# Fourier stage of a two-layer decoder kernel: VectorE reads a group's queries two units into the group, PE turns and projects the next group one unit sooner

## Chip, cores and metric

The kernel runs on one core of one Trainium2 chip. The metric is the device time of one execution in microseconds (us), as the median of several runs; lower is better. One further execution was taken with the hardware profiler, and all rows and views below come from that one.

## What is computed

A decoder of two layers on 64 sequences of 64 tokens of width 128. Layer 0 is self-attention, cross-attention and a mixture of experts, layer 1 is an attention with Fourier features, a latent cross-attention and a ternary feed-forward block; after each stands a layer norm over `x + branch(x)`. The change touches only the Fourier attention of layer 1, which has 16 heads of 8 numbers:

```
def _fourier_kernel(x, proj_mat):
    p = jnp.einsum('blhd,dm->blhm', x, proj_mat) / math.sqrt(D_HEAD)
    return jnp.concatenate([jnp.cos(p), jnp.sin(p)], axis=-1) / math.sqrt(D_KMAP)
q = (x @ Wq.T + bq).reshape(Bv, Lv, N_HEAD, D_HEAD)
k = (x @ Wk.T + bk).reshape(Bv, Lv, N_HEAD, D_HEAD)
v = (x @ Wv.T + bv).reshape(Bv, Lv, N_HEAD, D_HEAD)
q_prime = _fourier_kernel(q, proj_mat)
k_prime = _fourier_kernel(k, proj_mat)
kv = jnp.einsum('blhm,blhd->bhmd', k_prime, v)
out = jnp.einsum('blhm,bhmd->blhd', q_prime, kv)
out = out.reshape(Bv, Lv, D_MODEL)
return out @ Wo.T + bo
```

## The kernel before

The 4096 tokens stand in SBUF as 32 tiles of 128 tokens. The Fourier stage takes them in G = 8 groups of T = 4 tiles (512 tokens, that is 8 sequences). Each engine runs its own instruction list, written out in Python loops, and the lists meet only at semaphores; within an engine the order of the list is the order of execution.

The work of a group is cut into UPG = 16 **units** of 128 x 1024 angles: n = 0 to 7 (KEYS = 8) are the keys' features, n = 8 to 15 the queries'. All loops run over N = 16 g + n. For each unit the stations are:

- PE, `angles(N)` (L895 for keys, L897 for queries): the projection onto 128 random directions, into one of two pairs of PSUM banks. The PE loop issues it two units ahead, in iteration N - 2; it waits until VectorE has reduced unit N - 2, because that unit had the same banks.
- VectorE, `reduce_(N)`: the fractional part of the angle in turns. For ten units of a group this is `f_whole` (L1258), `f_frac` (L1266) and `f_wrap` (L1268). For the six units of `ON_SCALAR = (2, 5, 7, 10, 12, 14)` ScalarE rounds (`lift`, L1090, tile `f_lifted`), and VectorE does only `f_frac` (L1263) and `f_wrap`.
- ScalarE, `features(N)`: a sine (L1082) and a cosine (L1086). A `lift(N + 2)` stands between the two.
- PE again: `key_values` (L916) sums features times values over the keys' units, `turn_key_values` (L948) turns the sums, `outputs(g, q)` (L961) multiplies the queries' features with them, and `combine(g - 1)` (L975), in iteration n = 2 of the next group, is the output projection, which VectorE adds to the stream in `residual` (L1275) at n = 4.

Beside these, each group has to be prepared while the one before it is at work:

- `columns_of(g + 1)` on PE (L860): four transposes of the normalised tokens `f_xs` into bank 6, copied by ScalarE to `f_xT` (L1062). In both loops this stands at n = 11. After the transposes GpSimd is free to fill `f_xs` for the group after that (L1391) and to add the output bias to the stream (L1395).
- `keys_and_values(g + 1)` on PE at n = 12 (L867 and L869), read by VectorE after `reduce_` at n = 13: `keys` (`f_kT`, L1234) and `values` (`f_vS`, L1242).
- `queries(g + 1)` on PE at n = 14 (L874), behind `outputs(g, 2)`, read by VectorE after `reduce_` at n = 15 (`f_qT`, L1249). What `queries` writes is first used by PE in `angles` at n = 8 of group g + 1, which PE issues in its iteration n = 6:

```
if n == KEYS:
    pe.wait_ge(s["q_sb"], g + 1)
```

The keys' bank and the queries' bank are the same, bank 7; the next to write into it is `turn_key_values` at n = 6 of group g + 1, after that wait. SyncE has one DMA in the stage that depends on the queries: it waits until the last group's `queries` matmul has run, and then loads the first rows of the context into `f_xT`. Neither the DMA nor the matmul it waits for is touched.

In the names used below, unit (g, n) or "unit 13" is a unit of the loops above, and "reduced" means that `f_frac` of that unit is done.

Of the kernel before, what the change touches and what calls it, by code (L numbers as in the profile page):

```python
# [29 lines left out]
G = NT // T  # L30
# [679 lines left out]
def experts_and_fourier_phase(nc, ctx, c, name):  # L710
# [15 lines left out]
    KEYS = T * KU  # L726
# [42 lines left out]
    def x_bank(g):  # L769
        return XT if g == 0 else 6  # L770
# [22 lines left out]
    with nc.Block() as block:  # L793
# [8 lines left out]
        def _(pe):  # L802
# [50 lines left out]
            def columns_of(g):  # L853
                pe.wait_ge(s["staged"], g + 1)
                if g >= 1:
                    pe.wait_ge(s["kvT_sb"], 2 * g)
                else:
                    pe.wait_ge(e["xT_sb"], G)
                for t in range(T):
                    last = nc.tensor.transpose(ps[:, x_bank(g), t * P:(t + 1) * P], xs[:, t, :], ident)  # L860
                last.then_inc(s["xT_ps"], 1)
# [10 lines left out]
            def queries(g):  # L872
                pe.wait_ge(s["k_sb"], g + 1)
                nc.tensor.matmul(ps[:, k_bank(g), :], w("f_wq"), xT[:, :], start=True, stop=True).then_inc(s["q_ps"], 1)  # L874

            def angles(N):
                g, n = divmod(N, UPG)
                if n == 0:
                    pe.wait_ge(s["k_sb"], g + 1)
                if n == KEYS:  # L880
                    pe.wait_ge(s["q_sb"], g + 1)
                if N == 0:
                    pe.wait_ge(s["v_sb"], 1)
                    pe.wait_ge(s["q_sb"], 1)
                if N == 1:
                    pe.wait_ge(e["relued"], PIECES - 2)
                if N >= 2:
                    pe.wait_ge(s["reduced"], N - 1)
                for q in range(2):
                    out = ps[:, 2 * (N % 2) + q, :]  # L890
                    rows = slice(S * q, S * q + S)
                    if n < KEYS:
                        t, u = divmod(n, KU)
                        h = 8 * q + 4 * u
                        last = nc.tensor.matmul(out, kT[rows, t * P:(t + 1) * P], projX[rows, h:h + 4, :], start=True, stop=True)  # L895
                    else:
                        last = nc.tensor.matmul(out, projX[rows, n - KEYS + 8 * q, :], qT[rows, :], start=True, stop=True)  # L897
                last.then_inc(s["z_ps"], 1)

            def key_values(N):  # L900
                g, n = divmod(N, UPG)
                t, u = divmod(n, KU)
                if n == 0:
                    pe.wait_ge(s["v_sb"], g + 1)
                    if g >= 1:
                        pe.wait_ge(s["o_sb"], g * Q4 - 1)
                    else:
                        pe.wait_ge(e["relued"], PIECES)
                if n == 1 and g >= 1:
                    pe.wait_ge(s["o_sb"], g * Q4)  # L910
                if t == 2 and u == 0:
                    pe.wait_ge(s["kv_sb"], 2 * g + 1)
                pe.wait_ge(s["feats"], N + 1)
                for place in range(8 * u, 8 * u + 8):
                    q, r = divmod(place, 4)
                    last = nc.tensor.matmul(ps[32 * r:32 * r + 32, 4 + q // 2, (q % 2) * 256:(q % 2 + 1) * 256],  # L916
                                            vS[:, t % 2, t // 2, head_of(place), :],
                                            feats[:, n % RING, place % 2 * 4 + place % 8 // 2, :, :],
                                            start=(t % 2 == 0 and q % 2 == 0), stop=(t % 2 == 1 and q % 2 == 1))
                last.then_inc(s["kv_ps"], 1)  # L920
# [60 lines left out]
            for m in range(PIECES + 2):  # L981
                g, i = divmod(m, PARTS)
# [19 lines left out]
            for N in range(ALL + 5):  # L1002
                g, n = divmod(N, UPG)
                if N + 2 < ALL:
                    angles(N + 2)
                if g < G:
                    if 1 <= n <= KEYS:
                        key_values(N - 1)
                    if 3 <= N <= 6:
                        latent_products(N - 3)  # L1010
                    if n == (8 if g == 0 else 6):
                        turn_key_values(g, 0)
                    if n == 9:
                        turn_key_values(g, 1)
                    if n >= KEYS + 2 and n % 2 == 0:
                        outputs(g, n // 2 - 5)
                    if g + 1 < G:
                        if n == 11:
                            columns_of(g + 1)
                        if n == 12:  # L1020
                            keys_and_values(g + 1)
                        if n == 14:
                            queries(g + 1)
                if g >= 1:
                    if n == 0:
                        outputs(g - 1, Q4 - 1)
                    if n == 2:
                        combine(g - 1)

        @block.scalar  # L1030
        def _(act):
# [24 lines left out]
            def root(n, tiles):  # L1056
                act.wait_ge(e["variances"], n)
                nc.scalar.activation(rstd[:, tiles], rstd[:, tiles], ACT.Sqrt).then_inc(e["roots"], 1)
# [60 lines left out]
            for m in range(PIECES):  # L1119
                g, i = divmod(m, PARTS)  # L1120
# [11 lines left out]
            for N in range(ALL + 5):  # L1132
                g, n = divmod(N, UPG)
                if g < G:
                    if N == KEYS:
                        act.wait_ge(s["ab_ps"], 4)
                        act.wait_ge(e["lowered"], PIECES)
                        act.wait_ge(e["measured"], 2 * G)
                    if N == KEYS - 2:
                        root(3, LATE)  # L1140
                    features(N)
                    if 3 <= N <= 6:
                        keep_products(N - 3)
                    if n == 4:
                        keep_kv(g, 0)
                    if g == 0 and n == 8:
                        keep_turned(g, 0)
                    if n == 8:
                        keep_kv(g, 1)
                    if g >= 1 and n == 7:  # L1150
                        keep_turned(g, 0)
                    if n == 9:
                        keep_turned(g, 1)
                    if n >= KEYS + 3 and n % 2 == 1:
                        keep_o(g, (n - KEYS - 3) // 2)
                    if n == 11 and g + 1 < G:
                        columns_of(g + 1)
                if g == G and n == 0:
                    act.wait_ge(s["var"], 1)
                    nc.scalar.activation(c["rstd"][:, 0:MEASURED], c["rstd"][:, 0:MEASURED], ACT.Sqrt)  # L1160
                    nc.scalar.activation(rstdc[:, :], rstdc[:, :], ACT.Sqrt).then_inc(s["root"], 1)
                if g >= 1:
                    if n == 1:
                        keep_o(g - 1, Q4 - 1)
                if g == G and n == 2:
                    act.wait_ge(s["var2"], 1)
                    nc.scalar.activation(rstd2[:, 0:MEASURED], rstd2[:, 0:MEASURED], ACT.Sqrt).then_inc(s["root2"], 1)

        @block.vector
        def _(dve):  # L1170
# [76 lines left out]
            def queries(g):  # L1247
                dve.wait_ge(s["q_ps"], g + 1)
                nc.vector.tensor_scalar(qT[:, :], ps[:, k_bank(g), :], turn_scale, qb[:, :], ALU.mult, ALU.add).then_inc(s["q_sb"], 1)  # L1249
# [82 lines left out]
            for m in range(PIECES):  # L1332
                g, i = divmod(m, PARTS)
# [20 lines left out]
            for N in range(ALL + 6):  # L1354
                g, n = divmod(N, UPG)
                if N == 1:
                    e_residual(G - 1)
                if N == 3:
                    dve.wait_ge(e["measured"], 2 * G)
                    variance(LATE)  # L1360
                if N == KEYS:
                    inverse_of_root(3, LATE)
                if g == G and n == 0:
                    variances()
                    scales()
                    first_latents()
                if g < G:
                    reduce_(N)
                    if g + 1 < G:
                        if n == KEYS + 5:  # L1370
                            keys(g + 1)
                            values(g + 1)
                        if n == KEYS + 7:
                            queries(g + 1)
                if g >= 1 and n == 4:
                    residual(g - 1)

# [838 lines left out]
```

## Time and profile before

| | |
|---|---|
| median of 3 runs | 1605.61 us (1602.69 to 1608.95) |
| the profiled execution, its own time | 1600.41 us |
| its span, first to last instruction | 1598.6 us |
| mean granted TensorE clock | 0.969 of full speed |
| busy share of the span: PE, VectorE, ScalarE, GpSimd | 89%, 71%, 60%, 19% |
| Fourier stage | about 500 to 930 us |

The shares of the whole span mix five stages. The Fourier stage has to be read by itself: by the time from one group to the next, and by which engine waits for which inside a group. In the rows, an entry such as "[0.82 <-PE psum L867]" says that the engine sat idle for 0.82 us before this instruction until the PE instruction of line 867 released it. PE names TensorE's matmuls, PEld its weight loads, DVE is VectorE, ACT ScalarE, POOL GpSimd. In a timeline the printed durations of two neighbours overlap by some 0.1 us; the distance of two starts is the better measure. A row of busy times gives the stretch and its length, then for PE, PEld, DVE, ACT and POOL the busy microseconds with the number of instructions, then the mean granted TensorE clock, the DMA engines' busy share and GB/s.

### The profile page before, as it was taken

Reading aid. Unit: us, or ns where it says so; the run is one execution under the profiler, and the core shown is the slowest. Engines: PE = TensorE matmul, PEld = TensorE weight load, DVE = VectorE, ACT = ScalarE, POOL = GpSimd, SP = SyncE. Lnnn points to the kernel's source line nnn. Section 1 sums busy time; section 2 is a strip of 40 time slices with the busy share of each in tenths; the row PEclk is TensorE's granted clock in tenths of the full one; section 3 lists DMA queues with packets and bytes.
Section 4 is the critical chain, followed back from the end, with each engine's and each line's share of the span. In section 5 each row is a group of like instructions: output and inputs, shape, how many; then the busy total and the mean of one; then the engine's idle time right before and its main releaser. Section 6 shows DMA issues by size and latency. Waiting matters only on the chain. (4 is left out here: it accounts for less than half of the span.)

```text
span 1598.6 us, 32271 instructions
## 1 busy us (share of the span) xinstructions
PE 1420.6 (89%) x12643; PEld 867.7 (54%) x12658; DVE 1135.5 (71%) x2367; ACT 959.8 (60%) x1494; POOL 303.4 (19%) x278
## 2 busy tenths in 40 slices
PE   6999999997999788878887878999999999999962
PEld 4666666665665333334333354666666666666541
DVE  4666778886336799889988944355677767766788
ACT  2333367666555988789878954445666655565433
POOL 3434334452001100111010031111222111110101
PEclk9999999998999999999999989999999999999995
DMA  4000000001000000000000002222222222222310
GB/s 179 2 2 2 2 19 12 15 6 54 1 1 1 1 2 1 1 1 1 1 1 4 1 14 56 70 65 62 57 60 66 68 67 66 61 57 57 72 45 17
DMA packets 41013, 50.78 MB, mean 32 GB/s; under 512 B 9248, under 2 KB 23200, under 8 KB 40480
## 3 DMA queue, kind: packets, MB, share of 16 engines
q1 hardware_dynamic: 40576, 48.06, 11.7%
q8 instruction: 102, 1.67, 0.5%
q10 hardware_dynamic: 288, 0.67, 0.1%
q14 instruction: 47, 0.39, 0.1%
HBM read 13.04 MB, written 2.10 MB: 9 GB/s over the span
## 5 line engine op out<-in xcount | busy, mean ns | idle before, releaser
L1852 DVE TENSOR_TENSOR l_px<-psum,l_share 128x1024 f32<-128x1024 f32 x64 | 78.4, 1225 | 157.9 <-PE psum L1554 104.2
L1702 ACT ACTIVATE l_prob<-psum,l_bias 128x1024 f32<-128x1024 f32 x64 | 71.3, 1114 | 173.6 <-PE psum L1529 173.6
L1541 PE MATMUL psum<-l_XT,l_A 128*128 128x256 f32 x512 | 127.1, 393 | 1.0 <-ACT l_XT L1720 1.0
L1524 PE MATMUL psum<-l_th,l_XT 128*128 128x512 f32 x256 | 124.0, 607 | 1.9 <-issue 0.7
L1592 PE MATMUL psum<-l_px,l_N 128*128 128x256 f32 x512 | 124.0, 385 | 1.8 <-ACT l_r L1746 1.8
L1554 PE MATMUL psum<-l_prob,l_X 128*128 128x512 f32 x256 | 123.1, 603 | 0.0
L895 PE MATMUL psum<-f_projX,f_kT 64*128 64x512 f32 x256 | 75.2, 664 | 34.1 <-DVE f_frac L1266 18.6
L1592 PEld LDWEIGHTS psum<-l_px,l_N 128*128 128x128 f32 x512 | 93.9, 191 | 19.0 <-issue 4.7
L1833 DVE TENSOR_REDUCE l_top<-psum 128x8 bf16<-128x1024 f32 x64 | 78.1, 1221 | 36.4 <-PE psum L1609 36.4
L1541 PEld LDWEIGHTS psum<-l_XT,l_A 128*128 128x128 f32 x512 | 94.9, 195 | 12.4 <-ACT l_XT L1720 1.4
L1266 DVE TENSOR_TENSOR f_frac<-psum,f_whole 128x1024 f32<-128x1024 f32 x80 | 98.0, 1225 | 2.7
L1258 DVE TENSOR_SCALAR f_whole<-psum 128x1024 f32<-128x1024 f32 x80 | 97.4, 1217 | 1.8 <-PE psum L895 1.3
L2051 POOL TENSOR_TENSOR l_hn<-l_hh,late_weights 128x1024 f32<-128x1024 f32 x16 | 37.6, 2351 | 307.1 <-DVE l_hh L1910 307.1
L1707 ACT COPY l_th<-psum 128x1024 f32<-128x1024 f32 x64 | 64.8, 1012 | 47.7 <-PE psum L1541 47.7
L1268 DVE TENSOR_SCALAR f_wrap<-f_frac 128x1024 int32<-128x1024 int32 x128 | 89.9, 702 | 4.4
L408 ACT ACTIVATE a_probT<-psum 128x1024 f32<-128x1024 f32 x32 | 32.7, 1023 | 96.4 <-PE psum L199 96.4
L916 PE MATMUL psum<-f_feats,f_vS 128*32 128x256 f32 x1024 | 70.3, 393 | 15.1 <-ACT f_feats L1086 7.9
L961 PE MATMUL psum<-f_qf,f_kvm 128*32 128x256 f32 x1024 | 70.6, 422 | 13.3 <-ACT f_kvm L1114 6.7
L669 POOL TENSOR_TENSOR a_KX<-a_KT,const 128x1024 f32<-128x1024 f32 x32 | 60.8, 1903 | 113.6 <-ACT a_KT L375 89.5
L1082 ACT ACTIVATE f_feats<-f_frac 128x1024 f32<-128x1024 f32 x64 | 67.6, 1056 | 23.2 <-DVE f_frac L1266 23.2
L480 DVE TENSOR_TENSOR a_prob<-psum,relbias 128x1024 f32<-128x1024 f32 x32 | 39.2, 1225 | 55.6 <-PE psum L185 50.1
L399 ACT ACTIVATE c_QX<-c_QT,const 128x128 f32<-128x128 f32 x256 | 78.5, 403 | 0.0
(310 smaller groups left out, 3177.5 us busy)
## 6 DMA issues: line engine op xcount, KB each, us to landing
l_share<-l_recip SPq DMA_DIRECT2D x512, 64.0 KB, 2.0
early_weights<-in_weights SPq DMA_DIRECT2D x1, 2405.0 KB, 11.3
c_cs<-in_ctx SPq DMA_DIRECT2D x16, 128.0 KB, 2.1
f_qf<-in_l_mats SPq DMA_DIRECT2D x1, 2048.0 KB, 7.8
out<-l_normed SPq DMA_DIRECT2D x16, 128.0 KB, 2.0
l_craw<-in_ctx SPq DMA_DIRECT2D x15, 128.0 KB, 2.3
late_weights<-in_weights SPq DMA_DIRECT2D x1, 1089.0 KB, 11.2
relbias<-in_relbias ACTq DMA_DIRECT2D x1, 512.0 KB, 5.2
```

Source lines behind the costliest of these rows:

```text
L399: last = nc.scalar.activation(QX[:, n % 3, :, j, :], QT[:, d % DUOS, t * P:(t + 1) * P].rearrange("p (b s) -> p b s", s=S), ACT.Copy, scal ...
L895: last = nc.tensor.matmul(out, kT[rows, t * P:(t + 1) * P], projX[rows, h:h + 4, :], start=True, stop=True)
L1258: nc.vector.tensor_scalar(whole[:, :], z, MAGIC, MAGIC, ALU.add, ALU.subtract).then_inc(s["rounded"], 1)
L1266: nc.vector.tensor_tensor(frac[:, N % RING, :], z, whole[:, :], ALU.subtract).then_inc(s["reduced"], 1)
L1268: nc.vector.tensor_scalar(wrap[:, N % RING, :].bitcast(I32), frac[:, N % RING, :].bitcast(I32), 0x7FFFFFFF, None, ALU.bitwise_and).then_in ...
L1524: nc.tensor.matmul(ps[:, SC + n, :], XT[:, q % 3, k, :, :], th[:, q % 2, k, 8 * n:8 * n + 8, :], start=True, stop=False)
L1541: last = nc.tensor.matmul(ps[:, at + j // 2, (j % 2) * 256:(j % 2 + 1) * 256], A[:, QB * k + j, :], XT[:, q % 3, :, 1, :], start=True, sto ...
L1554: last = nc.tensor.matmul(ps[:, GA + n, :], X[:, q % 2, k, :], prob[:, b % 4, n, :], start=True, stop=True)
L1592: last = nc.tensor.matmul(ps[:, YB, 0:256], N[:, h, :], px[:, q % 2, h, :, :], start=(h == 0), stop=(h == H - 1))
L1702: nc.scalar.activation(prob[:, b % 4, :, :], ps[:, SC:SC + 2, :], ACT.Exp, bias=bias[:, b:b + 1]).then_inc(s["exped"], 1)
L1833: nc.vector.tensor_reduce(top[:, b % 4, :], ps[:, RO:RO + 2, :].rearrange("p a (j n) -> p (a j) n", n=P), AX.X, ALU.max, negate=True).then ...
L1852: nc.vector.tensor_tensor(px[:, q % 2, :, k, :], ps[:, GA:GA + 2, :].rearrange("p a (h s) -> p (a h) s", s=S), share[:, (b // 2) % 2, b % ...
```

## The change

Three pieces of work change their place; none is added, removed or resized.

- PE: `columns_of(g + 1)` goes from iteration n = 11 to the end of n = 10, and `keys_and_values(g + 1)` from n = 12 to n = 11. `queries(g + 1)` stays at n = 14.
- ScalarE: the copy to `f_xT` goes from n = 11 to n = 10.
- VectorE: `queries(g + 1)` (`f_qT`), which stood behind `reduce_` at n = 15 of group g, now stands behind `reduce_` at n = 2 of group g + 1, three units later. `keys` and `values` stay at n = 13. The `queries(0)` ahead of the loop stays.

```
@@ PE loop
                     if g + 1 < G:
+                        if n == 10:
+                            columns_of(g + 1)
                         if n == 11:
-                            columns_of(g + 1)
-                        if n == 12:
                             keys_and_values(g + 1)
                         if n == 14:
                             queries(g + 1)
@@ ScalarE loop
-                    if n == 11 and g + 1 < G:
+                    if n == 10 and g + 1 < G:
                         columns_of(g + 1)
@@ VectorE loop
                         if n == KEYS + 5:
                             keys(g + 1)
                             values(g + 1)
-                        if n == KEYS + 7:
-                            queries(g + 1)
+                if 1 <= g < G and n == 2:
+                    queries(g)
                 if g >= 1 and n == 4:
                     residual(g - 1)
```

## Rows read from the trace of the kernel before

**Rows 1.** Page, busy tenths of the span in 40 slices of 40 us
```profile
DVE  4666778886336799889988944355677767766788
```
**Rows 2.** Busy time by engine from one group's f_qT to the next, clock
```profile
559.00:609.70 50.70, 42.41 (x418) 19.35 (x418) 46.93 (x57) 43.87 (x48) 4.74 (x5) 1.00 0.01 2
...
662.10:715.90 53.80, 45.57 (x418) 20.42 (x418) 47.23 (x57) 43.92 (x47) 4.74 (x5) 0.94 0.01 1
...
sum 313.90, PE 264.29 PEld 119.21 DVE 281.97 ACT 264.97 POOL 23.71; mean PE 44.05 PEld 19.87 DVE 46.99 ACT 44.16 POOL 3.95
```
**Rows 3.** VectorE's waits, 500 to 900 us: in total, times, longest
```profile
DVE f_frac L1263 <- ACT f_lifted L1090: 15.4, 11, 2.4
DVE f_qT L1249 <- PE psum L874: 13.3, 8, 4.1
DVE f_kT L1234 <- PE psum L867: 5.9, 7, 1.0
```
**Rows 4.** Timeline of VectorE around a group's end: start, duration
```profile
595.57 1.22 DVE L1263 SCALAR_TENSOR_TENSOR f_frac<-f_lifted,psum 128x1024 f32<-128x1024 f32 x1 [1.31 <-ACT f_lifted L1090]
...
599.94 0.87 DVE L1268 TENSOR_SCALAR f_wrap<-f_frac 128x1024 int32<-128x1024 int32 x1
601.64 0.75 DVE L1234 TENSOR_SCALAR f_kT<-psum,f_kb 128x512 f32<-128x512 f32 x1 [0.82 <-PE psum L867]
...
608.66 0.69 DVE L1268 TENSOR_SCALAR f_wrap<-f_frac 128x1024 int32<-128x1024 int32 x1
609.74 0.75 DVE L1249 TENSOR_SCALAR f_qT<-psum,f_qb 128x512 f32<-128x512 f32 x1 [0.39 <-PE psum L874]
610.41 1.22 DVE L1258 TENSOR_SCALAR f_whole<-psum 128x1024 f32<-128x1024 f32 x1
...
617.89 0.69 DVE L1268 TENSOR_SCALAR f_wrap<-f_frac 128x1024 int32<-128x1024 int32 x1
618.50 1.22 DVE L1258 TENSOR_SCALAR f_whole<-psum 128x1024 f32<-128x1024 f32 x1
...
662.12 0.75 DVE L1249 TENSOR_SCALAR f_qT<-psum,f_qb 128x512 f32<-128x512 f32 x1 [2.02 <-PE psum L874]
```
**Rows 5.** Timeline of PE around the same group's end
```profile
595.68 1.13 PE L897 MATMUL psum<-f_qT,f_projX 64*128 64x512 f32 x4
596.74 0.66 PE L860 MATMUL psum<-const,f_xs 128*128 128x128 f32 x4
597.33 1.13 PE L897 MATMUL psum<-f_qT,f_projX 64*128 64x512 f32 x4
...
600.47 1.12 PE L867 MATMUL psum<-f_xT,early_weights 128*128 128x512 f32 x2
...
602.42 1.13 PE L897 MATMUL psum<-f_qT,f_projX 64*128 64x512 f32 x4
605.65 1.13 PE L895 MATMUL psum<-f_projX,f_kT 64*128 64x512 f32 x4 [2.10 <-DVE f_frac L1263]
...
612.94 1.13 PE L895 MATMUL psum<-f_projX,f_kT 64*128 64x512 f32 x4 [2.17 <-DVE f_frac L1266]
```
**Rows 6.** Timeline of ScalarE around the same group's end
```profile
596.44 1.08 ACT L1082 ACTIVATE f_qf<-f_frac 128x1024 f32<-128x1024 f32 x1
...
598.89 0.63 ACT L1062 COPY f_xT<-psum 128x512 f32<-128x512 f32 x1
...
600.32 1.07 ACT L1090 ACTIVATE f_lifted<-psum 128x1024 f32<-128x1024 f32 x1
...
625.00 1.02 ACT L1090 ACTIVATE f_lifted<-psum 128x1024 f32<-128x1024 f32 x1 [2.93 <-PE psum L895]
```
**Rows 7.** Timeline of GpSimd in the same group
```profile
597.50 3.45 POOL L1391 TENSOR_SCALAR f_xs<-stream,moments,rstd 128x128 f32<-128x128 f32 x4 [45.93 <-PE psum L860]
```
**Rows 8.** Busy time by engine, 3.4 us of low clock and 10 us of a group's middle
```profile
656.48:659.89 3.41, 3.41 (x20) 1.17 (x24) 3.34 (x4) 2.39 (x3) 0.00 (x0) 0.50 0.02 5
690.00:700.00 10.00, 7.83 (x84) 3.56 (x76) 8.62 (x9) 10.00 (x12) 0.00 (x0) 1.00 0.00 1
```

More of the change, by code:

```diff
@@ L1017, in _ @@
                     if g + 1 < G:
+                        if n == 10:
+                            columns_of(g + 1)
                         if n == 11:
-                            columns_of(g + 1)
-                        if n == 12:
                             keys_and_values(g + 1)
@@ L1155, in _ @@
                         keep_o(g, (n - KEYS - 3) // 2)
-                    if n == 11 and g + 1 < G:
+                    if n == 10 and g + 1 < G:
                         columns_of(g + 1)
@@ L1372, in _ @@
                             values(g + 1)
-                        if n == KEYS + 7:
-                            queries(g + 1)
+                if 1 <= g < G and n == 2:
+                    queries(g)
                 if g >= 1 and n == 4:
```

## The prediction

> **What bounds the kernel now.** I first read the busy shares and the slices of the page. VectorE is the one engine whose share has a ridge: in the slices from about 480 to 880 us it is busy seven to nine tenths, and elsewhere less [rows 1]. That is the Fourier stage. Then I cut that stage at the `f_qT` instructions, one cut a group. Six periods take 313.90 us together. Two of them are 50.7 us long at full clock and two 53.8 us at a mean clock of 0.94; the other two lie between. VectorE's work in each is the same, 46.9 to 47.2 us [rows 2]. So VectorE works 93% of a clean period, and a clean period can't go below about 47 us.
>
> The remaining 3.8 us are not all idle: each printed instruction has a few hundredths of a microsecond ahead of it. The real stalls stand in the list of waits [rows 3]: on `f_lifted` from ScalarE (15.4 us), on PE's queries (13.3 us, of which the longest, 4.1, is the one ahead of the stage's first unit) and on PE's keys (5.9 us, 7 times). The last two are what this change is about: 5.9 us, and 13.3 - 4.1 = 9.2 us.
>
> The chain inside one clean group, read across the three timelines, runs as follows. From `f_frac` of unit 12 (start 595.57) to unit 0 of the next group VectorE never waits for anything but those two reads [rows 4], while PE stands idle 2.10 and 2.17 us waiting for VectorE [rows 5]: VectorE sets the pace. From unit 0 on PE takes over. It has `angles` of unit 2, `outputs(g, 3)`, two `key_values` and `combine` to do, and only then `angles` of unit 5, for which ScalarE sits 2.93 us [rows 6]. From that `lift` on ScalarE has no gap up to unit 12 (10.00 us busy of 10.00 in such a stretch [rows 8]), and VectorE, which is ahead, waits 1.31 us for the `lift` of unit 12 [rows 4]. So the pace goes VectorE (units 12 to 0), PE (0 to 5), ScalarE (5 to 12). VectorE has room in the second and third stretch, none in the first.
>
> **The change part by part.** All in the clean group of rows 4 to 6; times are starts.
>
> *Keys.* PE now turns the columns after `outputs(g, 0)`, that is at 595.68 instead of 596.74; the four transposes take 597.33 - 596.74 = 0.59 us [rows 5]. So `angles` of unit 13 slips from 595.68 to 596.27 and ends at 597.33. VectorE needs it when its `f_wrap` of unit 12 ends, at 597.44: cover 0.1 us, and I charge 0.05. ScalarE copies at 596.44, right behind the cosine of unit 10 [rows 6]; the transposes end at 596.27, so no stall above 0.1. Sine and cosine of unit 11 slip by the copy's 0.47 us, and unit 12's sine is back in its old place, since the copy is gone from there. Keys and values follow on PE at 597.33 and last 602.42 - 600.47 = 1.95 us [rows 5], to 599.28; VectorE wants them at about 600.7. The wait is gone with 1.4 us to spare. What is pushed back is `angles` of unit 14, by 1.9 us to 599.28 to 600.35; ScalarE's `lift` of unit 14 started at 600.32 [rows 6], and so moves by 0.1 at most, and VectorE needs its result only behind keys and values. `outputs(g, 1)` and `angles` of unit 15 (602.2 against 602.42 [rows 5]) are where they were, since PE has done the same work by then.
> Gain: `f_kT` started at 601.64, and `f_wrap` before it is over at 599.94 + 0.87 = 600.81, less the 0.08 by which unhindered neighbours overlap (0.69 printed, next start 0.61 later at 617.89 and 618.50 [rows 4]): 600.73. **0.91 us a group.**
>
> *Queries, the wait.* `f_qT` started at 609.74 and the `f_wrap` before it at 608.66; without a wait the next start is 609.27. **0.47 us** in a clean group. In the others the wait is 2.02 instead of 0.39 [rows 4], 1.63 more; 3 x 0.39 + 4 x 2.02 = 9.25 is the 9.2 of rows 3, so four groups are of that kind.
>
> *Queries, the instruction.* `f_qT` takes 610.41 - 609.74 = 0.67 us out of the stretch in which VectorE sets the pace, and now stands between 617.89 and 618.50, behind unit 2. There PE sets it, through unit 5. Unit 0 comes 0.91 + 0.47 + 0.67 = 2.05 us sooner, PE and ScalarE follow by 2.05, and VectorE from unit 3 on by 2.05 - 0.67 = 1.38. That costs nothing until unit 12, where VectorE waited 1.31 and now waits 0.64. **0.67 us.** Were that cover gone, it would cost 0.67 a group and no more. Who waits for `f_qT`? Only `angles` of unit 8, four units later. Behind it on VectorE stands unit 3, whose reduction `angles` of unit 5 needs, but PE comes to that only after `combine`.
>
> *GpSimd.* The transposes release GpSimd 1.05 us sooner (597.50 [rows 7] becomes 596.45). It works 3.45 us on `f_xs` and then 1.28 us on the stream, and now lies beside two of VectorE's `f_wrap` (units 12 and 13) instead of one. The one that lay beside it took 0.87 instead of 0.69 us [rows 4]. I charge a second 0.18 us in the six groups that have this work: 1.1 us. The upper bound is that each of the two waits for one whole GpSimd instruction: 3.45 / 4 = 0.86 and 1.28, 2.1 us a group, 13 us in all. The lower is nothing.
> The Trainium skill ("SBUF — State Buffer", "Who interferes with whom") speaks against the change here: VectorE in a two-port mode and GpSimd exclude each other for a whole instruction. The trace shows 0.18 us where that rule could give up to 0.79, so the row decides; by the rule the result is the second rival below.
>
> *The clock.* In this stage the clock fell to 0.50, that is 1.2 GHz, for 3.4 us at a time [rows 8], and the two dips in the group at 662 come behind the places where PE had just been idle 2.10 and 2.17 us. The same gaps in clean groups had no dip, so they are enough in some positions only. After the change the first gap is from the end of `angles` of unit 15 (603.3) to 604.7, 1.4 us (605.65 - 0.91), and the second is 2.17 - (2.05 - 0.91) = 1.0 us. The idle time ahead of both dips falls by a third and by half, and I take it that the dips in the loop go. Their cost: 313.9 - 6 x 50.75 = **9.4 us**. The bounds are none of it (the dips stay) and all. If they stay, the four long waits for the queries go anyway: VectorE would let unit 2's angles start 0.91 + 2.10 + 0.67 = 3.7 us sooner, PE can do it 2.17 + 0.91 = 3.1 us sooner, so 4 x (1.63 - 0.6) = 4.1 us of the 9.4 are still gained.
>
> *Sum.* 7 x (0.91 + 0.47 + 0.67) = 14.4; less 7 x 0.05 and 1.1: 12.9; and the dips 9.4: **22.3 us less**. The last group and the hand-over to the next stage only come sooner. The profiled execution took 1600.4 us (span 1598.6), so one like it would take 1578. The median of the runs lies 5.2 us above it; the same gain gives **1583 us**.
>
> **Rivals.**
> A. *Part of it only: the dips stay or move.* For it: the clean groups show that position decides, and all positions move. Against it: the gaps shrink by 0.7 and 1.1. Gain 12.9 + 4.1 = 17, or 13 if the dips return everywhere: 1589 to 1593 us.
> B. *GpSimd in VectorE's way.* Each group loses up to 2.1 us more at units 12 and 13: 22.3 + 1.1 - 13 = about 10 us gained, 1595 us. For it: two wraps meet GpSimd now. Against it: the 0.18 us.
> C. *The change does nothing.* The keys' wait would stay if PE's transposes had to wait at n = 10. They wait for GpSimd's `f_xs`, which was ready a whole group before (45.93 us idle since [rows 7]), and for ScalarE's second turned copy, for which `outputs(g, 0)` ahead of them waits anyway. Or ScalarE turns out to set the pace all through, and VectorE's waits only move to `f_lifted`: then gain near 0, 1601 to 1609. Against it: ScalarE waited 2.93 us for unit 5.
> D. *Slower.* `keys_and_values` now stands ahead of `angles` of unit 14, `outputs(g, 1)` and `angles` of unit 15. If the copy to `f_xT` came late by x, all of them would stand behind the wait. VectorE needs unit 15 two instructions of 1.25 us ahead of its wrap, at 608.66 - 2.5 - 0.91 = about 605.2, and has it at 603.3: x up to 1.9 us is free. To eat the forecast's 22.3 / 7 = 3.2 a group and another 8 / 7 = 1.1, x must pass 6.2 us; it costs 1605.6 + 8 = 1614 us there. The copy is due at 596.9, 0.4 ahead of PE, and ScalarE's list has nothing before it that waits for PE's new work. Little chance.
>
> **How the numbers follow.** Forecast 0.60; A 0.17; B 0.10; C 0.08; D 0.05. A change of 0.5%, 8 us, is about what a measurement of this kernel can tell from none; the three runs spread over 6 us. The likeliest is 1583 us. The range takes in A and most of B above; below it the case that the unprofiled runs, 5 us longer, hold more dips than the profiled one and lose them all (another 8 us): 1574 to 1595. Faster by over 0.5%: the forecast, A, and most of B, 0.87. Within 0.5%: the rest of B and C, 0.09. Slower: 0.04.
>
> **What the changed profile would show.** No wait of `f_kT` or `f_qT` on PE inside the loop; seven `f_qT` behind the third reduction of a group. Clean groups 48.5 to 48.9 us from one unit 0 to the next, with VectorE's work still 46.9. The wait for `f_lifted` of unit 12 at about 0.65. PE's idle before `angles` of units 0 and 2 of the next group at 1.4 and 1.0 us instead of 2.1 and 2.2, and a clock of 1.00 in the groups. Two `f_wrap` of 0.87 us a group. The prediction is wrong if new waits on `f_lifted` of unit 14 or on angles of unit 13 stand in the list, if wraps beside GpSimd grow beyond 1 us, or if the clock dips as often as before.

## The result

The changed kernel takes 1577.46 us in the median of 4 runs (1570.12 to 1580.26), the kernel before 1604.15 us in the median of 4 runs beside them (1600.33 to 1608.95). The ratio of the runs is 0.9836, with a 95% interval from 0.9805 to 0.9868: 26.7 us, or 1.6%, faster. Forecast were 1583 us and a gain of 22.3. In a later set of runs the same kernel took 1573.57 us against 1603.95, ratio 0.9823 (0.9791 to 0.9854).

The two profiled executions lie closer together, 1600.41 and 1580.26 us: the first is at the fast end of its kernel's runs (the lowest is 1600.33), the second is the slowest of its four. What follows is therefore read group by group inside the stage, where the spacing repeats to 0.02 us, and not from the totals.

The spacing from one group's `f_qT` to the next, in the view of busy times by stretch. The columns are those of [rows 2].

```profile
567.00:615.30 48.30, 42.44 (x418) 19.40 (x416) 46.39 (x58) 43.88 (x48) 5.28 (x5) 1.00 0.01 1
...
808.50:856.80 48.30, 42.45 (x418) 19.40 (x416) 46.40 (x58) 43.89 (x48) 0.00 (x0) 1.00 0.01 4
sum 289.80, PE 254.64 PEld 116.39 DVE 278.36 ACT 263.32 POOL 26.41; mean PE 42.44 PEld 19.40 DVE 46.39 ACT 43.89 POOL 4.40
```

All six are 48.3 us long at a clock of 1.00. Before, there were 50.7, 52.4 and 53.8, 313.90 in sum [rows 2]: 24.1 us less in six groups. VectorE is now busy 46.4 of 48.3 us, 96% of a group. Its waits from 500 to 900 us, longest in total first:

```profile
DVE f_frac L1263 <- ACT f_lifted L1090: 13.4, 11, 2.8
DVE l_rstdc L1295 <- ACT l_rstdc L1161: 4.2, 1, 4.2
DVE f_qT L1249 <- PE psum L874: 4.1, 1, 4.1
DVE f_whole L1258 <- PE psum L895: 1.6, 2, 1.3
DVE rstd L1224 <- ACT rstd L1058: 1.6, 1, 1.6
```

Against [rows 3], `f_kT` is gone from the list, and `f_qT` is left with the one wait ahead of the loop. The second line, 4.2 us, belongs to the end of the stage and was there before too, behind 900 us. The timeline of VectorE around a group's end, beside [rows 4]:

```profile
594.81 1.22 DVE L1263 SCALAR_TENSOR_TENSOR f_frac<-f_lifted,psum 128x1024 f32<-128x1024 f32 x1 [0.88 <-ACT f_lifted L1090]
...
599.20 0.69 DVE L1268 TENSOR_SCALAR f_wrap<-f_frac 128x1024 int32<-128x1024 int32 x1
599.80 0.74 DVE L1234 TENSOR_SCALAR f_kT<-psum,f_kb 128x512 f32<-128x512 f32 x1
600.47 1.72 DVE L1242 SCALAR_TENSOR_TENSOR f_vS<-psum,f_vb 64x256 f32<-64x256 f32 x4
...
606.60 0.69 DVE L1268 TENSOR_SCALAR f_wrap<-f_frac 128x1024 int32<-128x1024 int32 x1
607.20 1.22 DVE L1258 TENSOR_SCALAR f_whole<-psum 128x1024 f32<-128x1024 f32 x1
...
615.30 0.74 DVE L1249 TENSOR_SCALAR f_qT<-psum,f_qb 128x512 f32<-128x512 f32 x1
```

From `f_frac` of unit 12 to unit 0 it is 12.39 us now (594.81 to 607.20) where it was 14.84 (595.57 to 610.41 in [rows 4]): 2.45 less. The group as a whole became 50.75 - 48.31 = 2.44 shorter. So the other 36 us of the group did not change, although `f_qT` now stands there. PE around the same place, beside [rows 5]:

```profile
594.91 0.66 PE L860 MATMUL psum<-const,f_xs 128*128 128x128 f32 x4
595.50 1.13 PE L897 MATMUL psum<-f_qT,f_projX 64*128 64x512 f32 x4
596.56 1.12 PE L867 MATMUL psum<-f_xT,early_weights 128*128 128x512 f32 x2
...
601.43 1.13 PE L897 MATMUL psum<-f_qT,f_projX 64*128 64x512 f32 x4
603.59 1.13 PE L895 MATMUL psum<-f_projX,f_kT 64*128 64x512 f32 x4 [1.03 <-DVE f_frac L1263]
...
609.74 1.13 PE L895 MATMUL psum<-f_projX,f_kT 64*128 64x512 f32 x4 [1.04 <-DVE f_frac L1266]
```

The two idle gaps of 2.10 and 2.17 us have become 1.03 and 1.04. The transposes stand ahead of unit 13's angles, and keys and values follow at once.

### The profile page after: what moved, and what is told of

Read it like the earlier page. It is cut to its first block and busy times, and to the rows that moved or that the text cites. A ratio compares the mean times of both kernels' runs of the same rounds, so it can differ in the third digit from the quotient of the medians.

```text
span 1578.4 us, 32271 instructions
## 1 busy us (share of the span) xinstructions
PE 1415.3 (90%) x12643; PEld 868.5 (55%) x12658; DVE 1132.3 (72%) x2367; ACT 959.6 (61%) x1494; POOL 306.6 (19%) x278
## 2 busy tenths in 40 slices
DMA packets 41013, 50.78 MB, mean 32 GB/s; under 512 B 9248, under 2 KB 23200, under 8 KB 40480
## 5 line engine op out<-in xcount | busy, mean ns | idle before, releaser
L897 PE MATMUL psum<-f_qT,f_projX 64*128 64x512 f32 x256 | 72.1, 639 | 9.8 <-DVE f_frac L1266 9.7
L1391 POOL TENSOR_SCALAR f_xs<-stream,moments,rstd 128x128 f32<-128x128 f32 x28 | 24.4, 881 | 266.5 <-PE psum L860 266.3
```

## The experiments

Each edit is shown against the kernel that the text names. The "group" is the distance between two `f_kT` of VectorE in the profile, without a dip of the clock unless said. Times are medians with the ratio to the kernel before, measured on the same chip. The totals of the variants that keep both edits lie between 1571.6 and 1579.9 us and, but for the two ends, can't tell them apart; the groups can.

### VectorE's queries alone

```
 # the kernel before, VectorE's loop
-                        if n == KEYS + 7:
-                            queries(g + 1)
+                if 1 <= g < G and n == 2:
+                    queries(g)
```

> The kernel before with one part of the change: VectorE reads the queries behind unit 2 of their group; PE's and ScalarE's lists are those of before. Theory (the two edits gain each for itself, the queries 0.47 us of wait and 0.67 us of instruction a clean group): a clean group 50.75 - 1.14 = 49.6 us, the wait for the keys still 0.82, PE's idle ahead of unit 0's angles still 2.1 and ahead of unit 2's about 1.0. With dips of the clock in some groups: 8 us for the seven groups and 4 to 8 us of dips, so 12 to 16 us faster. Rival (only PE's order counts, VectorE's reading moves a wait about): within 3 us of before, with a new or longer wait for f_lifted.

1588.08 us, ratio 0.9918 (0.9885 to 0.9951), which is 12.7 us less. Groups of 49.60 and 49.74 us in turn, the keys' wait still there:

```profile
600.28 0.75 DVE L1234 TENSOR_SCALAR f_kT<-psum,f_kb 128x512 f32<-128x512 f32 x1 [0.82 <-PE psum L867]
```

50.75 - 49.60 = 1.15 us, against 1.14 expected. This profile has dips of the clock, but they cost 0.14 us each:

```profile
604.30 1.35 PE L895 MATMUL psum<-f_projX,f_kT 64*128 64x512 f32 x4 [2.10 <-DVE f_frac L1263]
605.58 3.34 PE L961 MATMUL psum<-f_qf,f_kvm 128*32 128x256 f32 x32
608.85 1.13 PE L874 MATMUL psum<-f_xT,early_weights 128*128 128x512 f32 x2
```

The dip comes right behind the 2.10 us gap, as before, and makes `outputs` take 3.34 instead of 1.93 us. Yet VectorE no longer waits for the queries that come after it. So the late read also took most of the cost of a dip in this place off the path: 0.14 us is left of 1.63.

### PE's and ScalarE's order alone

```
 # the kernel after, VectorE's loop
+                        if n == KEYS + 7:
+                            queries(g + 1)
-                if 1 <= g < G and n == 2:
-                    queries(g)
```

> The kernel after, but with VectorE's queries behind unit 15 as before: only PE's and ScalarE's order is changed. Theory: the wait for the keys goes, 0.9 to 1.3 us a group, the wait for the queries of 0.39 stays (PE's queries come as much sooner as VectorE), so a clean group takes 49.4 to 49.8 us; PE's idle ahead of unit 2's angles stays 2.1 us, so that dips of the clock can still come. 7 to 15 us faster. Rival (the two edits need each other, since what is won at the keys is waited for at the queries): wait for the queries 1.3 to 1.7, clean group 50.7, no gain.

1592.74 us, ratio 0.9937 (0.9911 to 0.9963), which is 8.0 us less. One group takes 49.42 us, the other five 50.86 to 50.90. The clean one gains 50.75 - 49.42 = 1.33, at the upper end of what was expected. `f_qT` waits 0.39 in every group, as before: the queries on PE come sooner by as much as VectorE. The five long ones each hold a dip behind the gap ahead of unit 2's angles:

```profile
658.77 1.13 PE L895 MATMUL psum<-f_projX,f_kT 64*128 64x512 f32 x4
662.07 2.06 PE L895 MATMUL psum<-f_projX,f_kT 64*128 64x512 f32 x4 [2.17 <-DVE f_frac L1266]
664.06 2.63 PE L961 MATMUL psum<-f_qf,f_kvm 128*32 128x256 f32 x32
```

The angles of unit 2 take 2.06 instead of 1.13 us, `outputs` 2.63 instead of 1.93. The clean group has the same gap and no dip. A dip costs 50.87 - 49.42 = 1.45 us here, where PE sets the pace. The two edits therefore add up: 1.15 + 1.33 = 2.48, against 2.44 for both. And each of them closes one of the two gaps: with both, no dip is left between the first `f_kT` of the loop and the last, in either of the two profiles of the kernel after.

### GpSimd out of the way

```
 # the kernel before, GpSimd's loop
                 if g >= 1:
                     pool.wait_ge(s["xT_ps"], g)
                     pool.wait_ge(s["based"], g)
+                    if g >= 2:
+                        pool.wait_ge(s["q_sb"], g)
```

> The kernel before, in which GpSimd's work of a group waits until VectorE has read the queries, so that it no longer lies beside f_wrap of unit 13 and the values. Theory (GpSimd held VectorE up there): f_wrap of unit 13 takes 0.69 instead of 0.87, the distance from f_kT to f_vS 0.67 instead of 0.89, and a clean group is 0.2 us shorter; new slow instructions may show behind the queries. Rival (an f_wrap of 0.87 is one that is followed by a wait or differs for a reason of its own): both stay as they are, a clean group 50.75. In time less than 2 us either way.

1603.62 us, ratio 1.0013 (0.9993 to 1.0032), and clean groups of 50.75 and 50.78 us: nothing won, not even the 0.2 us a group of the theory. But one of the two rows moved as it says:

```profile
603.64 0.69 DVE L1268 TENSOR_SCALAR f_wrap<-f_frac 128x1024 int32<-128x1024 int32 x1
605.33 0.75 DVE L1234 TENSOR_SCALAR f_kT<-psum,f_kb 128x512 f32<-128x512 f32 x1 [1.00 <-PE psum L867]
606.22 1.73 DVE L1242 SCALAR_TENSOR_TENSOR f_vS<-psum,f_vb 64x256 f32<-64x256 f32 x4
```

`f_wrap` of unit 13 takes 0.69 instead of 0.87, so GpSimd had indeed slowed it; the wait behind it is 1.00 instead of 0.82, so the 0.18 had been covered. The distance from `f_kT` to `f_vS` stays 0.89, so it is not GpSimd's. In the kernel before, the values' matmuls on PE are over just as `f_vS` starts:

```profile
601.44 1.05 PE L869 MATMUL psum<-early_weights,f_xT 128*128 128x128 f32 x8
...
601.64 0.75 DVE L1234 TENSOR_SCALAR f_kT<-psum,f_kb 128x512 f32<-128x512 f32 x1 [0.82 <-PE psum L867]
```

They end at 602.49, and `f_vS` starts at 602.53. Where the values are ready long before, in the kernel after, the distance is 0.67. The list of waits shows the wait for the keys and not the 0.22 us for the values behind it.

### The queries behind unit 0, and behind unit 5

```
 # the kernel after, VectorE's loop; in the second kernel n == 5
-                if 1 <= g < G and n == 2:
+                if 1 <= g < G and n == 0:
```

> The kernel after, with the queries read behind unit 0 instead of unit 2. Theory (VectorE sets the pace up to unit 1: PE's angles of unit 3 start 0.02 us after unit 1 is reduced): unit 1 is reduced 0.67 us later and PE with all behind it comes 0.65 us later, a clean group 48.95 instead of 48.31, 4 to 5 us slower than the kernel after. Rival (PE sets the pace from unit 0 on, so any place behind it is free): 48.31 and the time of the kernel after.

1578.37 us, ratio 0.9856 (0.9825 to 0.9888). The group takes 48.95 to 48.96 us, 0.65 more than 48.31, to the digit what was expected of a PE that waits for VectorE's unit 1. So VectorE still sets the pace at unit 1. The total, 4 us more by the groups, doesn't stand out of the noise.

> The kernel after, with the queries read behind unit 5 instead of unit 2, the last place before PE's angles of unit 8 need them. Theory (between units 2 and 12 VectorE has room, 0.88 us of it left at the f_lifted of unit 12): a clean group stays at 48.31 us, the time that of the kernel after within the noise. Rival (the late read itself becomes a wait for PE's angles of unit 8): PE waits for f_qT, and a group grows by up to 1 us, 7 us in all.

1577.19 us, ratio 0.9852 (0.9818 to 0.9885). The group takes 48.31 us: the place is as good as unit 2's, and PE never waits for `f_qT`.

### One more instruction for VectorE, behind unit 3 and behind unit 14

```
 # the kernel after; in the second kernel "g + 1 < G and n == 14"
+    extra = sb("extra", [P, G])
...
+                if 1 <= g < G and n == 3:
+                    nc.vector.tensor_reduce(extra[:, g:g + 1], frac[:, N % RING, 0:512], AX.X, ALU.max)
```

> The kernel after with one more VectorE instruction in each of seven groups, behind unit 3: a maximum over 512 numbers into a small tile that nothing reads, 0.6 to 0.7 us. It leaves nothing of the computation out. Theory (VectorE has 0.88 us of room there): the f_lifted wait of unit 12 shrinks to 0.2 to 0.3 us, a clean group stays at 48.31 to 48.4. Rival (VectorE paces the whole group, being busy 97 per cent of it): 0.6 us more a group, 48.9 to 49.0, 4 to 5 us slower than the kernel after.

> The kernel after with the same additional VectorE instruction (a maximum over 512 numbers that nothing reads) behind unit 14. Theory (VectorE paces units 12 to 0): a clean group grows by the whole instruction, 48.31 + 0.6 to 0.7, and the f_lifted wait of unit 12 stays at 0.88; 4 to 5 us slower than the kernel after. Rival (it is absorbed by the slack ahead of unit 12): 48.31.

The groups of instructions by line, of the one behind unit 3 and of the one behind unit 14:

```profile
L1377 DVE TENSOR_REDUCE f_extra<-f_frac 128x1 f32<-128x512 f32 x6 | 4.1, 677 | 0.0
```

```profile
L1377 DVE TENSOR_REDUCE f_extra<-f_frac 128x1 f32<-128x512 f32 x6 | 4.1, 678 | 0.0
```

The same instruction of 0.68 us costs 48.43 - 48.31 = 0.12 us a group behind unit 3 and 48.89 - 48.31 = 0.58 us behind unit 14. In total 1574.38 (ratio 0.9848, 0.9813 to 0.9883) and 1577.89 us (0.9861, 0.9832 to 0.9891). By the distance of two starts the instruction holds VectorE for 0.60 us:

```profile
603.89 0.68 DVE L1377 TENSOR_REDUCE f_extra<-f_frac 128x1 f32<-128x512 f32 x1
604.49 1.21 DVE L1259 TENSOR_SCALAR f_whole<-psum 128x1024 f32<-128x1024 f32 x1
```

Behind unit 3, 0.45 of it went into the wait for unit 12's `f_lifted`, which is 0.43 instead of 0.88, and 0.12 into the group. Expected were a wait of 0.2 to 0.3 and a group of 48.31 to 48.4; why 0.12 reaches the group while room is left wasn't followed. Behind unit 14 the wait for unit 12 is 0.90, as good as unchanged. So an instruction's place in VectorE's list decides what an instruction costs, although VectorE is busy 96% of the time.

### Combine one iteration later

```
 # the kernel after, PE's loop and VectorE's
-                    if n == 2:
+                    if n == 3:
                         combine(g - 1)
...
-                if g >= 1 and n == 4:
+                if g >= 1 and n == 5:
                     residual(g - 1)
```

> The kernel after with combine of the group before in PE's iteration 3 instead of 2, behind the angles of unit 5, and VectorE's residual behind unit 5 instead of unit 4. Theory (PE's combine holds up the lift of unit 5, from which ScalarE paces up to unit 12): ScalarE's wait of 2.27 us for unit 5 goes, so does VectorE's wait of 0.88 for f_lifted of unit 12, and a clean group takes 47.4 to 47.6 us; 5 to 6 us faster than the kernel after, some 1572. Rival (the angles of unit 6 come too late behind combine, or the residual takes VectorE where it has no room): a new wait on unit 6 or 7, a group of 48.3 or more.

1579.93 us, ratio 0.9882 (0.9847 to 0.9917), and a group of 48.96 us: 0.65 longer, not 0.8 shorter. The theory named the right wait, which is gone, and not the next one. ScalarE's copy of the key-value sums now waits for PE, whose fourth `key_values` comes after combine:

```profile
622.65 1.01 ACT L1096 COPY f_kvs<-psum 128x1024 f32<-128x1024 f32 x1 [2.68 <-PE psum L916]
```

2.27 us at the `lift` became 2.68 at the copy. VectorE's wait for unit 12 grew from 0.88 to 1.30 instead of going away.

### Combine in two and in four pieces

```
 # the kernel after; in the second kernel {2: (0,), 3: (1,), 4: (2,), 5: (3,)} and 6 for 5
-            def combine(g):
+            def combine(g, tiles):
...
-                for t in range(T):
+                for t in tiles:
...
-                last.then_inc(s["y_ps"], 1)
+                if T - 1 in tiles:
+                    last.then_inc(s["y_ps"], 1)
...
-                    if n == 2:
-                        combine(g - 1)
+                    places = {2: (0, 1, 2, 3)} if g == G else {2: (0, 1), 3: (2, 3)}
+                    if n in places:
+                        combine(g - 1, places[n])
...
-                if g >= 1 and n == 4:
+                if g >= 1 and n == (4 if g == G else 5):
                     residual(g - 1)
```

> The kernel after with combine of the group before cut in two: tiles 0 and 1 in PE's iteration 2, tiles 2 and 3 in iteration 3, residual behind unit 5; the stage's last combine is left whole. Theory (combine's 3.7 us in one piece hold up ScalarE, at the lift of unit 5 by 2.27 us in the kernel after and at the copy of the key-value sums by 2.68 when combine stands one iteration later): in two pieces of 1.86 the first wait shrinks to about 0.5 and the second to about 1.0, ScalarE gains 0.8 us a group, the f_lifted wait of unit 12 goes from 0.88 to 0.1, a clean group takes 47.5 us; some 5 us faster than the kernel after. Rival (ScalarE is held up by the sum of both waits, 2.3 to 2.7, however combine is cut): a group of 48.3.

> The kernel after with combine cut in four, a tile in each of PE's iterations 2 to 5, residual behind unit 6; the last combine whole. Theory (ScalarE takes about 1 us a piece and more out of its own work): both waits of ScalarE under 0.5, VectorE paces the whole group, no f_lifted wait at unit 12, 47.4 us a group, 6 us faster than the kernel after and about the floor of 46.93 us of VectorE's work. Rival (the residual behind unit 6 is too late for turn_key_values, which waits for bank 6): PE waits there and ScalarE with it, a group of 48 us or more.

> The kernel after, unchanged, on the same chip as the two cut ones. Every theory: a group of 48.31 us in the profile. If single executions differ mainly by where the clock dips in the stages outside the Fourier stage, the time falls between 1570 and 1581 us like before.

| kernel | median us, 5 runs | ratio to before | group us |
|---|---|---|---|
| in two | 1571.61 | 0.9805 (0.9771 to 0.9839) | 47.83 |
| in four | 1576.38 | 0.9832 (0.9801 to 0.9863) | 48.30 |
| the kernel after, again | 1573.57 | 0.9823 (0.9791 to 0.9854) | 48.30 |

In two pieces the waits of ScalarE are as expected; VectorE's for unit 12 is 0.43, where 0.1 was expected:

```profile
615.25 1.02 ACT L1092 ACTIVATE f_lifted<-psum 128x1024 f32<-128x1024 f32 x1 [0.52 <-PE psum L895]
620.23 1.01 ACT L1098 COPY f_kvs<-psum 128x1024 f32<-128x1024 f32 x1 [0.94 <-PE psum L916]
```

The group gains 0.48 of the hoped-for 0.8 us. Over seven groups that is 3.4 us, and the medians on one chip stand 2.0 us apart, with intervals that overlap: the gain is shown in the groups, and in the total only in its direction. In four pieces the sum of both waits is gone from ScalarE's list, but combine's last piece comes too late for VectorE, which sits idle for the residual in each of the six groups in view:

```profile
DVE stream L1277 <- PE psum L975: 3.8, 6, 0.6
DVE f_frac L1265 <- ACT f_lifted L1092: 1.0, 6, 0.2
```

Expected were 47.4 us a group; the rival's number, 48 or more, came true, and not its reason: PE has no new wait at `turn_key_values`. That the wait for the residual is what makes up the 0.47 us against two pieces is likely and wasn't tested by itself.

## Why the prediction was right

**The pace of the three stretches** (VectorE from unit 12 to 0, PE to 5, ScalarE to 12) is what the forecast rests on, and it held but for one border: the extra instruction costs 0.58 behind unit 14 and 0.12 behind unit 3, and the queries cost nothing behind units 2 and 5. But behind unit 0 they cost 0.65, where PE should have had the pace already. VectorE keeps it through unit 1. The change was safe from this because it puts `f_qT` behind unit 2.

**Queries, wait and instruction**, 0.47 + 0.67 = 1.14 a group: 1.15 measured alone.

**Keys**, 0.91 a group less 0.05 for unit 13's angles and 0.18 for GpSimd, 0.68: 1.33 measured alone. All three terms were mis-sized, each to the disfavour of the change. (a) The 0.22 us that `f_vS` waited for the values' matmuls were overlooked; they show only as the distance of two starts, 0.89 against 0.67 now. (b) The charge for unit 13 is nothing: 1.87 us from `f_frac` of unit 12 to `f_whole` of unit 13 in both kernels. (c) GpSimd costs VectorE nothing more: all `f_wrap` in the stage take 0.69 or 0.70, and the 0.18 us taken from the keys' gain for a slow wrap came back with it. These add up: 0.68 + 0.22 + 0.05 + 2 x 0.18 = 1.31. It is GpSimd that got slower:

```profile
595.68 3.55 POOL L1391 TENSOR_SCALAR f_xs<-stream,moments,rstd 128x128 f32<-128x128 f32 x4 [42.94 <-PE psum L860]
599.31 1.73 POOL L1395 TENSOR_TENSOR stream<-f_xs,early_weights 128x512 f32<-128x512 f32 x1
```

They took 3.45 and 1.28 before. (The prediction's 3.45 / 4 = 0.86 us for one instruction of the first was a mean over unlike ones: three take 0.79 and the one beside `f_wrap` 1.13.) So rival B is refuted by row, and the "two `f_wrap` of 0.87 us a group" with it.

**The clock**, 9.4 us from dips that were to go: all gone between the first `f_kT` and the last, in both profiles of the kernel after. The gaps were forecast at 1.4 and 1.0 and are 1.03 and 1.04; the first is off by the 0.22 and the 0.18 us of (a) and (c). That the length of a gap matters, and not only its place, is borne out by the other kernels. With one edit alone one long gap is left, and dips only behind it. A gap between the two lengths was followed by none: seven of 1.41 us with combine in two, seven of 1.44 with combine later, and seven with the extra instruction behind unit 14, such as

```profile
610.14 1.13 PE L896 MATMUL psum<-f_projX,f_kT 64*128 64x512 f32 x4 [1.63 <-DVE f_frac L1267]
```

Why a gap of 2.1 us has a dip behind it in one group and none in the next stays open, as in the prediction. For dips that stay behind the first gap the prediction left 0.6 us each of the 1.63; with the late read alone it was 0.14. Rivals A and C are refuted by the six groups of 48.3.

**The sum.** From the first `f_qT` to the last residual the stage took 930.07 - 499.64 = 430.43 us and takes 906.81 - 500.39 = 406.42: 24.0 us less, against 22.3. By terms: six groups at 2.44, 14.6, and the 9.4 of dips; the seventh keys and queries gained 2.4 more. They are gone again at the stage's two ends, outside the groups that were changed. From the first `f_qT` to `f_frac` of unit 12 in the first group it is 46.11 us and was 45.19: the clock is low there for 6.8 us at one go, and was low for 3.4 us twice. From the last `outputs` to the last residual it is 9.31 and was 7.75; PE's last combine has a dip:

```profile
901.02 5.74 PE L975 MATMUL psum<-early_weights,f_oT 128*64 128x128 f32 x64 [0.69 <-ACT f_oT L1102]
```

5.74 us instead of 3.71, less 0.47 us that the `outputs` ahead of it gained on its own dip of before. That makes 14.6 + 9.4 + 2.4 - 0.9 - 1.6 = 23.9. The profiled execution reached the stage 0.75 us later than before and needed 3.1 us more behind it, which leaves a span 20.2 us shorter. So it is in part luck that 24.0 lies so near to 22.3: seven groups gained 17.1 us without the dips, where the forecast had 12.9, and dips at the ends, of which the forecast had none, took 2.5 back. The median is 26.7 us lower; its interval is 21.2 to 31.3 and has 22.3 in it. What makes the runs of one kernel spread over some 10 us wasn't settled. Other variants' profiles show dips of the clock outside the loop in other places, and groups that repeat to 0.02 us, which speaks for the dips.

**Rival D** had its place right and no effect: the copy to `f_xT` starts at 595.68 right behind the transposes, and PE's keys follow without a gap.

What the prediction said would be seen and wasn't: clean groups of 48.5 to 48.9 us are 48.3, by the terms of the keys above. The wait for unit 12's `f_lifted`, about 0.65 by the prediction, is 0.88: VectorE is 0.24 us further ahead of ScalarE there than reckoned, and why wasn't followed.

## What to carry to other kernels

Ask of each stretch of a loop which engine sets its pace, and move what has a free choice of place out of the stretches of the busy engine into those in which it leads. A share of 96% doesn't mean that no such place is left. When a long block stands in an engine's list, moving it moves the wait to whoever is next behind it; cutting it helps only as long as its result isn't late itself. And where an engine's short gaps are followed by a slow clock, closing them can get rid of the slow clock as well: here 9.4 of 24 us.

## What the runs showed of the hardware that wasn't expected

A dip to 1.2 GHz, 3.4 us long, came behind PE gaps of 2.10 and 2.17 us, in some groups and not in others of the same kernel: behind four of the seven gaps of 2.10 and two of the seven of 2.17 in the kernel before, behind six of the seven of 2.17 with PE's order alone. Behind gaps of 1.63 us and less there was none between the first `f_kT` and the last, in any profile. At the stage's end the low clock once went on through a gap of 1.41 us (combine in four, at 895 us), but it had begun before that gap. Whether it cost 0.14, 1.45 or 1.63 us went with who waited for PE then.

Where an `f_wrap` of VectorE and an instruction of GpSimd meet, one or both take longer, and it is not always the one that began later. `f_xs` is four instructions of 0.79 us each when nothing disturbs them. The one that meets an `f_wrap`, in the kernel before (first line) and in the kernel after, and the `f_wrap` beside the latter:

```profile
599.83 1.13 POOL L1391 TENSOR_SCALAR f_xs<-stream,moments,rstd 128x128 f32<-128x128 f32 x1
...
595.68 1.22 POOL L1391 TENSOR_SCALAR f_xs<-stream,moments,rstd 128x128 f32<-128x128 f32 x1 [42.94 <-PE psum L860]
596.06 0.69 DVE L1268 TENSOR_SCALAR f_wrap<-f_frac 128x1024 int32<-128x1024 int32 x1
```

Before, the `f_wrap` began 0.11 us after GpSimd's instruction, and both grew, by 0.18 and 0.34 us. Now it begins 0.38 us after it, keeps its 0.69, and the earlier one grows by 0.43. GpSimd's addition to the stream, which begins 0.11 us after an `f_wrap` now, took 1.73 instead of 1.28 us. The Trainium skill ("SBUF — State Buffer", "Who interferes with whom") has issue order decide who blocks, and the other wait for the whole instruction. By the profile's starts this trace agrees for the addition, and in size nearly, 0.45 of a possible 0.58 us; it doesn't for the `f_xs` of now, which began first and lost.
